# Causal attention in quads: scores of two quads at a time in row tiles, one spread of the keys per sequence, one block of value matmuls, two probability copies on DVE

## The reference

```
x = x + _L0_attn_ref(_layernorm(x, axis=-1), L0_attn_w_qkv, L0_attn_b_qkv, L0_attn_w_out, L0_attn_b_out)

def _L0_attn_ref(x, w_qkv, b_qkv, w_out, b_out):      # H = 16 heads, Dh = 8
    qkv = x @ w_qkv.T + b_qkv
    q, k, v = jnp.split(qkv, 3, axis=-1)
    ...
    q, k = _rope(q, k)
    scores = jnp.einsum('bhtd,bhsd->bhts', q, k) / jnp.sqrt(jnp.float32(Dh))
    scores = jnp.where(causal, scores, -jnp.inf)
    probs = jax.nn.softmax(scores, axis=-1)
    out = jnp.einsum('bhts,bhsd->bhtd', probs, v)
    out = out.transpose(0, 2, 1, 3).reshape(b, t, d)
    return out @ w_out.T + b_out
```

## Time and profile before

| | us |
|---|---|
| median of three runs | 3467.15 |
| lowest and highest | 3467.04, 3475.69 |
| the profiled execution, its own time | 3479.02 |
| its span | 3477.2 |
| first stage, from the first score to the last sequence | about 21 to 636 |

### The profile page before, as it was taken

The page is one execution under the profiler, slowest core; times in us unless marked ns, Lnnn a source line. Parts: engine busy times, 40 slices in busy tenths (PEclk is TensorE's granted clock), DMA queues, the critical chain, the costliest instruction groups (busy, mean ns, idle before and its releaser), DMA issues. The chain is left out here.

```text
span 3477.2 us, 97864 instructions
## 1 busy us (share of the span) xinstructions
PE 3171.6 (91%) x27203; PEld 2330.7 (67%) x27357; DVE 2570.1 (74%) x8326; ACT 2244.4 (65%) x8816; POOL 1567.5 (45%) x2572
## 2 busy tenths in 40 slices
PE   7999999899999999999999986879979999967776
PEld 4666666688888888888888864657756666644443
DVE  7888888577777777777777761126657888879997
ACT  6888888566666666666666652327758999952221
POOL 6888888312222222222222210016647777746665
PEclk9999999899999999999999998989999999977677
DMA  4000000100000000000000002220000000000000
GB/s 144 0 0 0 0 0 0 75 4 6 5 5 5 5 5 5 5 5 5 5 5 5 4 4 67 79 61 17 17 10 6 5 5 5 5 2 11 7 12 18
DMA packets 80366, 54.39 MB, mean 16 GB/s; under 512 B 24801, under 2 KB 74413, under 8 KB 80160
## 3 DMA queue, kind: packets, MB, share of 16 engines
q1 hardware_dynamic: 76192, 45.27, 4.6%
q0 software_dynamic: 4096, 8.16, 0.8%
HBM read 32.67 MB, written 20.97 MB: 15 GB/s over the span
## 5 line engine op out<-in xcount | busy, mean ns | idle before, releaser
L897 DVE COPY b_prT<-b_tr 128x512 f32<-128x512 f32 x512 | 352.2, 688 | 236.6 <-PE b_tr L789 232.3
L1155 ACT ACTIVATE b_pr<-b_sc,b_low 128x205 f32<-128x205 f32 x1024 | 430.3, 430 | 34.3 <-DVE b_low L873 34.3
L478 ACT ACTIVATE a_pr<-a_sc,a_low 128x128 f32<-128x128 f32 x1024 | 364.2, 381 | 37.2 <-POOL a_pn L522 26.3
L1212 POOL TENSOR_TENSOR b_ln_var<-b_ln_mean_var,all_eps 128x1 f32<-128x1 f32 x64 | 12.0, 187 | 756.6 <-DVE b_ln_mean_var L140 756.6
L888 DVE TENSOR_SCALAR b_pn<-b_pr,b_rec 128x205 f32<-128x205 f32 x1024 | 298.4, 334 | 54.8
L789 PE MATMUL b_tr<-all_ident,b_pn 128*128 128x128 f32 x2048 | 322.4, 280 | 5.3 <-DVE b_prT L897 3.1
L2132 ACT ACTIVATE f_pr<-f_sc,f_low 128x77 f32<-128x77 f32 x1024 | 319.1, 335 | 10.9 <-DVE f_low L2023 2.9
L513 POOL TENSOR_TENSOR a_kx<-a_qk,w_hsel 128x512 f32<-128x512 f32 x256 | 291.7, 1151 | 2.4 <-DVE a_qk L349 2.4
L789 PEld LDWEIGHTS b_tr<-all_ident,b_pn 128*128 128x128 f32 x2048 | 226.6, 140 | 86.9 <-issue 79.3
L265 PE MATMUL a_sc<-a_kx,a_qk 128*128 128x512 f32 x512 | 262.3, 594 | 11.7 <-POOL a_kx L513 9.2
L873 DVE TENSOR_REDUCE b_low<-b_sc 128x4 f32<-128x820 f32 x256 | 256.4, 1002 | 10.2 <-PE b_sc L777 10.2
(11 more groups left out here) (292 smaller groups left out, 8795.4 us busy)
## 6 DMA issues: line engine op xcount, KB each, us to landing
scratch_x<-b_zeros SPq DMA_DIRECT2D x12, 512.0 KB, 5.0
e_xr<-scratch_x SPq DMA_DIRECT2D x24, 256.0 KB, 3.0
scratch_y<-e_yr SPq DMA_DIRECT2D x24, 256.0 KB, 2.4
all_X<-in_x SPq DMA_DIRECT2D x8, 512.0 KB, 6.9
e_w<-in_e_w SPq DMA_DIRECT2D x16, 256.0 KB, 3.0
out_x<-all_X SPq DMA_DIRECT2D x8, 512.0 KB, 3.2
w_mask<-in_mask SPq DMA_DIRECT2D x1, 2464.0 KB, 9.8
b_cT<-in_ctxT SPq DMA_DIRECT2D x32, 77.0 KB, 2.0
```

The source lines that it names most:

```text
L478: op = act.activation(pr[:, u % 2, g], sc[:, u % 2, 128 * g:128 * g + 128], ACT.Exp, bias=low[:, u % 2, g:g + 1], scale=-1.0, accum_out=su ...
L897: dve.tensor_copy(prT[:, j % 2, i].rearrange("p h t q -> p (h t q)"), tr[:]).then_inc(prT_made, 1)
L1155: op = act.activation(pr[:, j % 2, g, 0:KN], sc[:, j % 2, h, KN * i:KN * i + KN], ACT.Exp, bias=low[:, j % 2, g:g + 1], scale=-1.0, accum_ ...
```

## The change

Head 4g + u is the same, but the unit of work is now the quad g: its four heads lie in the 32 neighbouring features 32g to 32g + 31. `spread_keys` makes one 128 x 512 tile per sequence (`own` keeps, in copy u, the features whose head is 4g + u). `score(b, p, half)` lays down two masks and then scores the quads 2 half and 2 half + 1 in two row tiles of 32 features each. `sc` gets four buffers, `tr` only one, `prT` holds all four quads of two sequences. `values` is one block of 16 matmuls per sequence. All four divisions are on POOL (`divide`), the copies of quads 1 and 3 on DVE (`copy_odd`), those of 0 and 2 on ACT (`copy_even`). The orders of all four engines are rewritten. `hsel` is no longer loaded for this stage; `own` is a load of the same kind that the silu stage has too.

```
-                def score(b, p, u):
-                    n = 4 * b + u
-                    if due(n - 1):
-                        pe.wait_ge(exped, n - 1)
+                def score(b, p, half):
+                    n = 4 * b + 2 * half
+                    if due(n - 2):
+                        pe.wait_ge(exped, n - 2)
                     pe.wait_ge(roped, b + 1)
-                    pe.wait_ge(kx_made, n + 1)
-                    pe.matmul(sc[:, u % 2], consts.ident_bf[:], mask[:], start=True, stop=False)
-                    pe.matmul(sc[:, u % 2], qk[:, p, 0], kx[:, p, u], start=False, stop=True).then_inc(scored, 1)
+                    pe.wait_ge(kx_made, b + 1)
+                    for g in (2 * half, 2 * half + 1):
+                        pe.matmul(sc[:, g], consts.ident_bf[:], mask[:], start=True, stop=False)
+                    for g in (2 * half, 2 * half + 1):
+                        q = slice(32 * g, 32 * g + 32)
+                        last = pe.matmul(sc[:, g], qk[q, p, 0], kx[q, p].rearrange("p u k -> p (u k)"),
+                                         start=False, stop=True, tile_position=(32 * g, 0))
+                    last.then_inc(scored, 2)
...
+                def transposes(b, g):
+                    n = 4 * b + g
+                    pe.wait_ge(normed, n + 1)
+                    if g % 2:
+                        pe.wait_ge(prT_even, 2 * b + g // 2 + 1)
+                    elif due(n):
+                        pe.wait_ge(prT_odd, 2 * b + g // 2)
...
+                def values(b, p):
+                    pe.wait_ge(prT_even, 2 * b + 2)
+                    pe.wait_ge(prT_odd, 2 * b + 2)
+                    pe.wait_ge(vx_made, b + 1)
+                    if due(b):
+                        pe.wait_ge(oT_made, b)
+                    for u in range(NU):
+                        for g in range(NG):
+                            q = slice(32 * g, 32 * g + 32)
+                            last = pe.matmul(po[q, 0:128], vx[:, p, u, q], prT[:, p, g, u],
+                                             start=u == 0, stop=u == NU - 1, tile_position=(0, 32 * g))
                     last.then_inc(pv_made, 1)
...
+                def copy_odd(b, p, g):
+                    if due(b - 1):
+                        dve.wait_ge(pv_made, b - 1)
+                    dve.wait_ge(tr_made, 4 * b + g + 1)
+                    dve.tensor_copy(prT[:, p, g].rearrange("p u k -> p (u k)"), tr[:]).then_inc(prT_odd, 1)
...
+                def spread_keys(b, p):
 
                     pool.wait_ge(roped, b + 1)
-                    if due(4 * b - 8 + u + 1):
-                        pool.wait_ge(scored, 4 * b - 8 + u + 1)
-                    pool.tensor_tensor(kx[:, p, u], qk[:, p, 1].unsqueeze(1).broadcast_to([128, NG, 128]),
-                                       hsel[:, NG * u:NG * u + NG].unsqueeze(2).broadcast_to([128, NG, 128]),
-                                       ALU.mult).then_inc(kx_made, 1)
-
-                def divide_even(b, u):
-                    n = 4 * b + u
+                    if due(4 * b - 4):
+                        pool.wait_ge(scored, 4 * b - 4)
+                    pool.tensor_tensor(kx[:, p], qk[:, p, 1].unsqueeze(1).broadcast_to([128, NU, 128]),
+                                       own[:].unsqueeze(2).broadcast_to([128, NU, 128]), ALU.mult).then_inc(kx_made, 1)
+
+                def divide(b, g):
+                    n = 4 * b + g
```

More of the change, by code:

```diff
@@ L189, in stage_causal_attention @@
         mem = Memory(nc, ctx, "a")
-        wT, woT, bias, bv, bo, rope, mask32, hsel = tiles
+        wT, woT, bias, bv, bo, rope, mask32, own = tiles
         mask = mem.sbuf("mask", [128, NG, 128], BF16)
@@ L267, in transposes @@
-                def transposes(b, p, u):
-                    n = 4 * b + u
[L269 to L276, removed]
-                    last.then_inc(tr_made, 1)
@@ L297, in step @@
                 def step(b, p, last):
-                    first = isinstance(b, int) and b == 0
-                    ahead = not isinstance(b, int) or b + 2 < B
-                    if not last:
+                    transposes(b, 0)
+                    if inside(b + 1):
                         project_v(b + 1)
[L302 to L317, removed]
+                    if inside(b - 1):
+                        values(b - 1, 1 - p)
+                    transposes(b, 1)
+                    if inside(b + 1):
+                        score(b + 1, 1 - p, 0)
+                    transposes(b, 2)
+                    if inside(b + 2):
+                        transpose_x(b + 2, p)
+                    if inside(b + 1):
+                        score(b + 1, 1 - p, 1)
+                    transposes(b, 3)
+                    if inside(b - 1):
+                        project_out(b - 1)
+                    if inside(b + 2):
+                        project_qk(b + 2)
                     if last:
-                        values(b, p, NU - 1)
+                        values(b, p)
                         project_out(b)
@@ L327, in _ @@
                 project_qk(1)
-                for u in range(3):
-                    score(0, 0, u)
+                score(0, 0, 0)
+                score(0, 0, 1)
                 over_sequences(pe, step, tail=4)
@@ L402, in step @@
                 def step(b, p, last):
[L404 to L410, removed]
                     if isinstance(b, int) and b == 1:
@@ L414, in step @@
                         norm_statistics(dve, ln, X[:, b + 3], b + 3, 1 - p)
+                    invert(b, 2)
                     if inside(b + 1):
-                        lowest(b + 1, 0)
                         spread_values(b + 1, 1 - p)
@@ L419, in step @@
                         norm_moments(dve, ln, 1 - p)
+                    copy_odd(b, p, 1)
+                    if inside(b - 1):
+                        copy_out(b - 1)
+                    if inside(b + 1):
+                        lowest(b + 1, 0)
                     invert(b, 3)
-                    divide_odd(b, 3)
                     if inside(b + 1):
                         lowest(b + 1, 1)
+                    if inside(b + 3):
+                        dve.wait_ge(xT_made, b + 2)
+                        norm_apply(dve, ln, X[:, b + 3], b + 3, 1 - p)
+                    if inside(b + 1):
+                        lowest(b + 1, 2)
+                        invert(b + 1, 0)
+                    copy_odd(b, p, 3)
+                    if inside(b + 1):
+                        lowest(b + 1, 3)
+                        invert(b + 1, 1)
                     if inside(b - 1):
@@ L452, in _ @@
                 rotate(1, 1)
-                for u in range(3):
-                    lowest(0, u)
-                    if u == 0:
-                        invert(0, 0)
+                for g in range(NG):
+                    lowest(0, g)
+                invert(0, 0)
+                invert(0, 1)
                 over_sequences(dve, step, tail=4)
@@ L500, in _ @@
+                def step(b, p, last):
+                    exponentials(b, 2)
+                    copy_even(b, p, 0)
+                    exponentials(b, 3)
+                    if inside(b + 1):
+                        exponentials(b + 1, 0)
+                    copy_even(b, p, 2)
+                    if inside(b + 2):
+                        copy_xT(b + 2)
+                    if inside(b + 1):
+                        exponentials(b + 1, 1)
                 copy_xT(0)
```

151 lines of the change are left out of this document (59 added, 92 removed).

## The result

The changed kernel takes 3695.44 us (median of four runs, 3692.39 to 3704.25), the kernel before, measured beside it, 3469.34 (3467.04 to 3475.69): a ratio of 1.0649, 95% interval 1.0631 to 1.0667. It is slower by 226 us. Forecast was 3621, +154, with a range of 3540 to 3700: the sign and the range held, the size was 74 us short.

A forecast was written before the change was run, and what follows sets the result against it. PE was taken to bound the kernel before, at 9.61 us a sequence; after, a ring of waits of 11.6 plus 0.5 for the clock gives 12.1. Over 62 sequences that adds 154 to 3467.15: 3621 us, range 3540 to 3700.

The forecast's parts named there:

- The bound before, and the change of bound: First stage: PE bound before at 9.3 us a sequence; after, about 7.5, with waits instead of any engine setting the period.
- PE busy 60 to 65%: Sign expected in the after profile: PE's busy share in the first stage, causal attention.
- The ring: Chain of waits from transposes(b,1) to transposes(b+1,1) through PE, DVE, ACT and POOL, closing once per sequence: 11.6 us.
- ring without the clock: Rival: period 11.6 us in the first stage with no clock fall, +123, 3590 us; chance 0.22.
- The pair of row tiles: PE's scores in the first stage: two quads in row tiles take 0.95 us, between bounds 0.86 and 1.07.
- The rival of a pair that does not overlap: Rival: each score tile on PE takes its 0.86, +0.76 on the ring, period 12.9, 3671 us; chance 0.04.
- The values block and the idle stretch: Values on PE hides beside the ring, its saving returning nothing; PE idles some 2.5 us ahead of transposes(b+1,1).
- The clock: PE's idle piece lowers its clock in about one sequence in three, some 1.7 us each: 0.5 us a sequence.
- one in every sequence, 1.7: Upper bound of the clock term: one fall of PE's clock in each sequence of the first stage, costing 1.7 us.
- 0.85 to 0.98: Sign expected in the after profile: PE's granted clock in the first stage.
- Faster, because DVE sets the period: Rival: the ring does not bind; DVE, busiest at 7.6 us, sets the first stage's period, 3343 us; chance 0.08.
- A fall in each sequence, 3696: Rival: the ring with PE's clock falling every sequence, period 13.3 us, +229, 3696 us; chance 0.12.

The follow-up runs named there:

- The experiment without the clock loss: Changed kernel plus 16 bf16 matmuls that nothing reads, filling PE's idle time at the head of `values`; 3589.95 us, ratio 1.0337.
- the new orders: Changed kernel, same instructions, with the orders of all four engines rewritten, rotation moved up as well; 3443.46 us, ratio 0.9915.
- the opened ring: Changed kernel with POOL's spread of the keys of b+2 moved behind divide(b+1,1); 3493.21 us, ratio 1.0070.

## Why the prediction was right, and where it fell short

**The bound before, and the change of bound.** Right that no engine sets the period. DVE, ACT and POOL are busy 7.62, 7.04 and 6.22 us a sequence against forecasts of 7.5, 6.8 and 6.7. PE's 9.3 us became 7.99 (in a sequence of 11.27 at full clock) and not 7.5. Some 0.2 of that miss are the two pairs, which are 2.1 before the change into tiles is added, where 2.1 was the sum with it. The forecast of "PE busy 60 to 65%" was wrong as a thing to look for: it is 71% in a clean sequence, 7.99 of 11.27 where I had 7.5 of 12.1, and 80% over 500 us, since PE at half clock counts as busy for nearly twice as long (a pair 2.08 instead of 1.13). A high busy share beside a low clock is no sign of a bound engine.

**The ring.** Right in every member, and in its length to 3%. Taken from the starts in the timeline above, in the prediction's order:

| step of the ring | forecast | measured |
|---|---|---|
| transposes(b,1), masks, pair, to DVE | 2.14 | 2.20 |
| lowest, to ACT | 0.73 | 0.72 |
| exponentials, copy_even(b,2), to PE | 2.19 | 2.05 |
| transposes(b,3), to DVE | 0.66 | 0.76 |
| copy_odd(b,3), lowest, reciprocal, residual | 1.74 | 1.46 |
| rotation, to POOL | 1.83 | 1.91 |
| spread and division, to PE | 2.29 | 2.17 |
| sum | 11.6 | 11.27 |

The largest single miss is DVE's row: the copy, the minimum, the reciprocal and the residual start 0.61, 0.59, 0.09 and 0.17 apart, less than their busy times by more than I allowed. The ring was worth 102 us where 123 was summed for it. The experiment without the clock loss, 3590 us, has the very number of the rival "ring without the clock"; the agreement is partly luck, since its period is 0.3 shorter, and filling and draining make up the difference.

**The pair of row tiles.** Sized at 0.95, measured 1.06 from its start to the next work (335.28 to 336.34), outside none of the bounds (0.86 and 1.07) but at the upper one: a pair costs what four tiles cost in the earlier trace rows. Two of the experiments repeat the 1.06: 307.00 to 308.06 with the fill, 305.74 to 306.80 with the new orders. The choice "two lies between one and four" was wrong. By the span model of the Trainium skill ("TensorE: Matmul & The Clock Gate", Part 3) a pair would be 0.87, hardly more than a single matmul; the trace has 1.06 here, and the measurement decides. By the same model of the Trainium skill four tiles would be 0.87 too, an estimate, and the earlier trace rows already had 1.07: that row agrees with the page's speed-up, as the prediction says, but not with its span. On the ring it mattered by 0.06 in all. The rival of a pair that does not overlap (1.72) is out.

**The values block and the idle stretch.** Right that values is off the ring (1.83 us added there cost nothing), and right that the idle piece is some 2.5 us (2.43) and stands ahead of transposes(b+1,1). Ahead of `project_v` it is 0.16, not 0.5. The block runs from 342.01 to 343.09, beside the rotation, and not while POOL spreads keys (from 343.36) as forecast; nothing hangs on that.

**The clock.** This is the step that failed. Its mechanism was right, the term mis-sized: 0.5 us a sequence forecast, 1.85 measured, which is (1.85 - 0.5) x 62 = 84 us; the shorter ring took 20 of them back. That is 64 of the miss of 74; the rest lies outside the 62 sequences and their mean (226 us measured against 217 from the periods). Both factors were too small. How often: one sequence in three was taken, 17 of 33 were lengthened. How much: 1.7 us was taken for each, the mean is 1.85 x 33 / 17 = 3.6. So the bound "one in every sequence, 1.7" was no bound, and the stage's granted clock of 0.78 lies below the 0.85 to 0.98 that was forecast. That the range held is in part luck: its upper end was drawn from that bound, and 3695 lies 5 us under it.

The price can be read in the sequence from 319.29 to 334.26 of the kernel after, all at 1.2 GHz until its last third:

```profile
319.29 0.99 PE L272 MATMUL a_tr<-all_ident,a_pn 128*128 128x128 f32 x4 [1.96 <-POOL a_pn L505]
...
321.06 2.08 PE L260 MATMUL a_sc<-a_kx,a_qk 32*128 32x512 f32 x4
...
323.19 0.69 DVE L362 TENSOR_REDUCE a_low<-a_sc 128x4 f32<-128x512 f32 x1 [1.98 <-PE a_sc L260]
...
325.18 2.08 PE L260 MATMUL a_sc<-a_kx,a_qk 32*128 32x512 f32 x4
...
325.30 0.61 ACT L469 ACTIVATE a_prT<-a_tr 128x512 f32<-128x512 f32 x1
...
327.19 1.11 PE L272 MATMUL a_tr<-all_ident,a_pn 128*128 128x128 f32 x4
...
328.41 0.69 DVE L377 COPY a_prT<-a_tr 128x512 f32<-128x512 f32 x1 [0.33 <-PE a_tr L272]
...
330.18 1.13 DVE L335 SCALAR_TENSOR_TENSOR a_turn<-a_pf,w_bias,w_rope 128x128 f32<-128x128 f32 x4 [0.22 <-PE a_pf L239]
```

Step by step against the clean one: transposes to pair 1.77 for 1.02 (+0.75), pair to minimum 2.13 for 1.18 (+0.95), these two being the doubled work that I priced. Then what I did not see: from the copy on ACT (325.30) to transposes(b,3) it is 1.89 us instead of 0.66 (+1.23). At full clock the second pair hides beside ACT's exponentials; at half clock PE is still in it (from 325.18) when the copy is done, and it comes onto the path. Transposes(b,3) to the copy +0.46, and the rotation waits for `project_qk`, which is late too, +0.31. Sum 3.70, which is 14.97 - 11.27. I had taken the 4 us of the earlier trace rows and called their loss the cost of one fall. The two windows of the kernel before that follow there are these:

```profile
2078.00:2080.00 2.00, 1.05 (x10) 0.94 0.00 0
2080.00:2082.00 2.00, 0.00 (x0) 0.92 0.00 0
```

The clock was back in the first of them, PE's work ended in it, and nothing waited for PE in a ring. So these rows could tell that a fall comes, and not what it costs a loop whose work goes on: here it went on at 1.2 GHz for some 10 us.

**The rivals.** "Faster, because DVE sets the period" did not come: no engine was full. The rule of the Trainium skill that it leaned on ("TensorEngine Tiling (Array Packing)", PSUM Bottleneck), that the emptying of PSUM may become the bound once tiling has sped up TensorE, did not bind in any run here: with the best orders the period is 9.03, and DVE is busy 359 of 450 us, 7.2 a sequence. "A fall in each sequence, 3696" is near the measured time by number, but not by mechanism: 17 of 33 sequences at 3.6 us, not all at 1.7.

## What to carry to other kernels

In a loop whose engines each have a fixed order, go once round before you believe the sums of busy time: from one instruction to the same one a step later, through every queue in which it is stuck behind something else. Where that way is longer than the busiest engine, the period is its length; PE was relieved of 1.3 us here and the loop still got 1.7 longer, and exchanging two lines in POOL's queue took most of it back. And where such a ring leaves TensorE idle for a microsecond or two in each turn, price the clock with the whole step at half speed, with the work in it that only hid before.

## What the runs showed of the hardware

- In a loop that repeats every 11 to 15 us, with a PE idle piece of 1.6 us in each turn a drop from 2.4 to 1.2 GHz lengthened 5 of 37 turns, with one of 2.4 us 17 of 33; with pieces of up to 1.08 us there was none (fill of 16, and the opened ring). The idle time of the whole turn grew along with the piece. The low clock lasted some 10 us (305 to 316, 320 to 330) while PE had work.
- Sixteen matmuls that nothing reads, put into PE's idle piece, made the changed kernel 105 us faster: the clock stayed at 1.00.
- Two row tiles of 32 x 512 f32 cost as much as four of them, 1.06 and 1.07 us.
- Queues at a fixed clock repeat closely: 39 periods in a row within 0.02 us, with no engine full.
